# Prologue of a cross-attention and mixture-of-experts kernel: an order of its own for each engine, and fp32 raw scores for the first unit

## The chip, the cores and the metric

The kernel runs on one core of a Trainium2 chip. Its time is the device time of one execution in microseconds (us), the median over several runs. TensorE is the matrix engine (PE in the profile, PEld its weight loads), VectorE is DVE, ScalarE is ACT, GpSimd is POOL, and SyncE (SP) issues most of the DMAs. Rows whose engine ends in q (SPq, ACTq) are instructions that issue DMAs.

## What is computed

The input `x` is 8 x 256 x 512, with `ctx` of the same shape and a mask of 8 x 512. Cut to what matters:

```
y = x + attention(layernorm(x), ctx)   # 16 heads of 16 dims over the 256 channels, 512 positions
    q = Wq @ ln(x) + bq;  k = Wk @ ctx + bk;  v = Wv @ ctx + bv
    dot = q.T @ k / 4;  dot = mask * dot - (1 - mask) * 1e6
    out = (softmax(dot) * mask) @ v
out = y + experts(layernorm(y))        # 8 experts, top 2 by a gate; silu(g) * u, then w2
```

## The kernel before

The attention works on 16 **units** of 128 channels (8 heads of 16 dims), two to a batch. A unit goes through a pipeline: load `x`, normalize, project queries and keys (fp32 matmuls into a PSUM tile, `project`, line 1017), add bias and mask (`projection_out`, line 812, into `qkf`), and split each fp32 value in three bf16 **parts** (GpSimd's `part`, lines 554 to 562). The parts go out to `stack_d` in DRAM (`keep_split`, line 370) and come back **stacked** (`stack`, lines 352 and 355) in `qk`, so that one bf16 matmul over 97 rows gives a raw score in nearly full precision, the mask row among them. `raw_scores` (line 985) fills a tile of two such matmuls, and VectorE takes the maximum of each row (`maximum`, line 731). A unit has 16 such tiles, `m` 0 to 15. TensorE transposes the maxima (line 1072), VectorE splits them in three rows (lines 742 to 748), and SP writes these into `qk` (line 454). Then the real scores follow (`scores`, line 972, 100 rows), ScalarE takes the exponential (line 629), and `product` (line 1001) multiplies by the values (`values`, line 1028). Head by head, unit u+1's maxima are taken while unit u's scores run.

Each engine has its own program, and every one of them is the same loop: `unit(u)` for `u` from `FIRST` = -5 to `LAST` = 18, in which the parts that have no unit yet are left out. In iteration `u`, TensorE runs unit u's scores in eight steps `s`, the raw scores of unit u+1 from `m` = 4 on and of unit u+2 for `m` < 4, values of unit u+1 after step 1, queries of unit u+3 after step 3 and keys of unit u+3 after step 7. Raw scores for `m` = 0 stand in step 6, and `m` = 8 in step 2 of the next iteration; each waits for one half of the unit's stack. PSUM tiles come from a ring of two (`NSLOT`), so that a tile waits until the one two before it is read. The list `TILES` gives their order and the numbers that semaphores count.

Iterations -5 to -1 are the prologue. There GpSimd first fills constant ones (lines 486 and 488), waits for all 13 constant loads, and only then takes its first reciprocal root (lines 534 and 536). VectorE and TensorE wait likewise for all constants. SP writes padding rows of 1.3 MB (lines 468 and 470) between its iterations -3 and -2. The experts come after the attention, and lines above 1110 are theirs.

## Time and profile before

| | us |
|---|---|
| median of 3 runs | 930.77 (930.25 to 931.76) |
| profiled execution | 934.06 |
| its span, first to last instruction | 932.3 |

The attention ends near 620 us and the experts take the rest. In the rows below a timeline line gives the start and the length in us, then engine, line, operation, output<-input, the number of instructions merged, and in brackets how long the engine idled before and what ended that. Busy time is pipelined for TensorE, so the starts of neighbouring matmuls tell more than their lengths.

### The profile page before, as it was taken

Reading aid. Unit: us, or ns where it says so; the run is one execution under the profiler, and the core shown is the slowest. Engines: PE = TensorE matmul, PEld = TensorE weight load, DVE = VectorE, ACT = ScalarE, POOL = GpSimd, SP = SyncE. Lnnn points to the kernel's source line nnn. Section 1 sums busy time; section 2 is a strip of 40 time slices with the busy share of each in tenths; the row PEclk is TensorE's granted clock in tenths of the full one; section 3 lists DMA queues with packets and bytes.
Section 4 is the critical chain, followed back from the end, with each engine's and each line's share of the span. In section 5 each row is a group of like instructions: output and inputs, shape, how many; then the busy total and the mean of one; then the engine's idle time right before and its main releaser. Section 6 shows DMA issues by size and latency. Waiting matters only on the chain. (4 is left out here: it accounts for less than half of the span.)

```text
span 932.3 us, 12897 instructions
## 1 busy us (share of the span) xinstructions
PE 804.5 (86%) x3737; PEld 368.1 (39%) x3738; DVE 543.6 (58%) x1038; ACT 316.7 (34%) x615; POOL 376.7 (40%) x396
## 2 busy tenths in 40 slices
PE   2177999999999999999999888219999999999994
PEld 1022333333333333333333232216666666665662
DVE  2167878887888888887778772232333333323332
ACT  0002565556565555655566567000000000000000
POOL 4634354557556655755575142410122222212122
PEclk9667999999999999999999999559999999999998
DMA  4553386667666765856564423242465455463342
GB/s 122 169 171 94 120 246 185 205 190 231 197 208 208 235 197 172 278 153 188 169 204 148 115 83 104 103 148 47 69 159 131 88 147 116 113 160 68 68 68 34
DMA packets 84287, 137.69 MB, mean 148 GB/s; under 512 B 14600, under 2 KB 40520, under 8 KB 84240
## 3 DMA queue, kind: packets, MB, share of 16 engines
q1 hardware_dynamic: 68512, 107.97, 38.5%
q0 software_dynamic: 7744, 17.86, 10.1%
q10 hardware_dynamic: 7984, 11.28, 4.3%
q8 instruction: 23, 0.38, 0.2%
q14 instruction: 24, 0.20, 0.1%
HBM read 77.34 MB, written 59.36 MB: 147 GB/s over the span
## 5 line engine op out<-in xcount | busy, mean ns | idle before, releaser
L731 DVE TENSOR_REDUCE mx<-tile 128x2 f32<-128x1024 f32 x256 | 308.7, 1216 | 67.4 <-PE tile L985 63.8
L629 ACT ACTIVATE pr<-sc 128x512 f32<-128x512 f32 x512 | 268.9, 601 | 193.3 <-PE sc L972 190.5
L985 PE MATMUL tile<-qk 97*128 97x512 bf16 x512 | 158.1, 392 | 49.3 <-DVE mx L731 23.6
L972 PE MATMUL sc<-qk 100*128 100x512 bf16 x512 | 155.1, 383 | 7.4 <-DMA qk<-mxt 4.8
L1289 POOL DMA_INDIRECT out_dram<-y,ids x36 | 56.1, 1558 | 259.7 <-DVE ids L1210 255.7
L1001 PE MATMUL pvb<-pr,vp 128*32 128x512 f32 x1024 | 138.0, 611 | 0.0
L985 PEld LDWEIGHTS tile<-qk 97*128 97x128 bf16 x512 | 36.4, 98 | 189.2 <-DVE mx L731 84.0
L1269 ACT ACTIVATE sg<-gp 128x352 f32<-128x352 f32 x36 | 16.7, 463 | 266.5 <-PE gp L1310 266.5
L1342 PE MATMUL dp<-wring,at 128*128 (+1 forms) x216 | 98.8, 593 | 1.7 <-DVE at L1220 1.7
L1310 PE MATMUL gp<-wring,xtile 128*128 x288 | 93.5, 468 | 1.1 <-DVE meta L1201 1.1
L554 POOL TENSOR_SCALAR parts<-qkf 128x512 bf16<-128x512 f32 x32 | 48.4, 1511 | 110.8 <-DVE qkf L812 109.9
L1310 PE MATMUL up<-wring,xtile 128*128 x288 | 91.2, 459 | 0.0
L972 PEld LDWEIGHTS sc<-qk 100*128 100x128 bf16 x512 | 49.5, 100 | 91.0 <-ACT pr L629 39.0
L1310 PEld LDWEIGHTS gp<-wring,xtile 128*128 128x128 f32 x288 | 55.6, 193 | 41.9 <-issue 19.3
L1226 DVE TENSOR_SCALAR y<-dp,metay 128x512 f32<-128x512 f32 x36 | 27.0, 751 | 71.4 <-PE dp L1342 71.4
L1310 PEld LDWEIGHTS up<-wring,xtile 128*128 128x128 f32 x288 | 51.9, 190 | 22.8
L1342 PEld LDWEIGHTS dp<-wring,at 128*128 128x128 f32 (+1 forms) x216 | 41.0, 190 | 43.8 <-issue 36.3
L1235 DVE TENSOR_TENSOR ac<-sg,up 128x352 f32<-128x352 f32 x36 | 18.8, 521 | 55.4 <-PE up L1310 29.8
L1017 PE MATMUL tile<-xh,wq_s 128*128 128x512 f32 x64 | 34.3, 662 | 18.8 <-DVE xh L674 17.9
L559 POOL TENSOR_SCALAR parts<-rest 128x512 bf16<-128x512 f32 x32 | 47.7, 1491 | 2.8
L1218 DVE COPY at<-atp 128x256 f32<-128x256 f32 x36 | 15.3, 424 | 55.2 <-PE atp L1332 49.0
L569 POOL TENSOR_TENSOR att<-num,rb 128x512 f32<-128x512 f32 x16 | 20.3, 1268 | 59.7 <-DMA rb<-recip_d 59.7
(118 smaller groups left out, 745.2 us busy)
## 6 DMA issues: line engine op xcount, KB each, us to landing
qk<-stack_d SPq DMA_DIRECT2D x32, 768.0 KB
stack_d<-parts SPq DMA_DIRECT2D x32, 384.0 KB, 2.6
wring<-w_dram SPq DMA_DIRECT2D x32, 352.0 KB, 6.2
xl<-routed_d ACTq DMA_DIRECT2D x38, 257.0 KB, 2.7
stack_d<-parts SPq DMA_DIRECT2D x32, 256.0 KB, 2.9
pv_d<-ov SPq DMA_DIRECT2D x32, 256.0 KB, 4.3
xin<-x_dram SPq DMA_DIRECT2D x16, 256.0 KB, 5.4
cin<-ctxt_dram SPq DMA_DIRECT2D x8, 512.0 KB, 6.4
```

Source lines behind the costliest of these rows:

```text
L554: pool.tensor_scalar(parts[:, side, 0, :], src, 1.0, None, ALU.mult).then_inc(done.sem, 1)
L559: pool.tensor_scalar(parts[:, side, 1, :], rest[:, side, :], 1.0, None, ALU.mult).then_inc(done.sem, 1)
L629: nc.scalar.activation(pr[s % 2][:, j, :], sc[(32 * u + 4 * s + j) % NSC][:, :], ACT.Exp, scale=SCALE).then_inc(exped.sem, 1)
L731: dve.tensor_reduce(mx[:, half(w), 2 * j:2 * j + 2], t[:, :, :], X, ALU.max, negate=True).then_inc(drained.sem, 1)
L972: nc.tensor.matmul(sc[(32 * u + 4 * s + j) % NSC][:, :], ks[half(u)][0:ALL_ROWS, h, c * P:c * P + P], qs[half(u)][0:ALL_ROWS, h, :], start ...
L985: last = nc.tensor.matmul(t[:, i, :], qs[half(w)][0:RAW_ROWS, h, c * P:c * P + P], ks[half(w)][0:RAW_ROWS, h, :], start=True, stop=True)
L1001: last = nc.tensor.matmul(pvb[32 * i:32 * i + 32, :], vp[half(u)][:, c, 4 * g + i, :], pr[s % 2][:, i, :], start=(c == 0), stop=(c == 3))
L1017: last = nc.tensor.matmul(t[:, 0, :], weight[:, c, half(w) * P:half(w) * P + P], source[:, parity(w), c, :], start=(c == 0), stop=(c == 1))
L1226: dve.tensor_scalar(y[:, k, :], dp[:, :], metay[:, k, 0:1], None, ALU.mult).then_inc(y_made, 1)
L1289: pool.indirect_dma_start(out, bass.IndirectOffsetOnAxis(ap=ids[:, k, :], axis=0), y[:, k, :], None, compute_op=ALU.add).then_inc(y_added, 16)
L1310: last = nc.tensor.matmul(dst[:, 0:I], xt[k][:, c, :], wring[:, bass.ds(off + (c * 2 * I + o), I)], start=(c == 0), stop=(c == 3))
L1342: last = nc.tensor.matmul(dp[:, :], at[0:w, c, :], wring[0:w, bass.ds(off + (W1N + c * T), T)], start=(c == 0), stop=(c == len(ICHUNKS) - 1))
```

## The change

The loop from `FIRST` to -1 is replaced, on every engine, by a list written out by hand. The constants that are needed first (`early`) are loaded first, with semaphores of their own, and each engine waits for these alone. Queries and keys of units 0 and 1 are projected one after another. The queries and keys of unit 0 are copied in fp32, a head to each group of 32 partitions, with a mask row below (`heads_in`, into `qf`, which lies in the buffer `pr0`). The raw scores of unit 0 come from these (`first_raw`): 17 rows of fp32 each, two heads to a tile. Meanwhile GpSimd splits the queries of unit 0, and VectorE the keys (`key_parts`), and they are stacked for the real scores as before. The queries and keys of unit 2 are projected inside iteration 0, after steps 0 and 2. The padding rows are written after iteration 1.

```
+        max_ = [(n, ("max", m)) for m in pairs_of(n, s)]
+        ev += max_[:1]
+        if s == 7 and has(n - 2):
+            ev.append((n, "ranks"))
+        ev += max_[1:]
+        ev += [(n, name) for name in fillers(n, s)]
+        if n == 0 and s == 0:
+            ev.append((-1, "q"))
+        if n == 0 and s == 2:
+            ev.append((-1, "k"))
...
+FIRST_TILES = ([(-3, "q"), (-3, "k"), (-2, "q"), (-2, "k")] + [(-2, ("max", m)) for m in range(LEAD)]
+               + [(-1, ("max", m)) for m in range(LEAD, NPAIR)] + [(-1, "maxT"), (-1, ("max", 0)), (-1, ("max", 1)),
+               (-1, "v"), (-1, ("max", 2)), (-1, ("max", 3))])
+TILES = FIRST_TILES + [tile for n in range(LAST + 1) for tile in tile_events(n)]
...
+        qf = pr[0][:, :, :].rearrange("p (g s) t -> p g s t", g=2)
+        mf = ge[:, :, :].rearrange("o a b -> o (a b)")[:, 0:2 * T].rearrange("o (s t) -> o s t", s=2)
...
+        early = ((io[:, :], iotas, io_in),
+                 (wq_s[:, :, :], wq.rearrange("(c p) o -> p c o", p=P), wq_in),
+                 (bqk[:, 0, :], bq, wq_in),
+                 (wk_s[:, :, :], wk.rearrange("(c p) o -> p c o", p=P), wk_in),
+                 (bqk[:, 1, :], bk, wk_in),
+                 (mall[:, :], mask, mask_in))
...
+        def heads_in(eng, heads):
+
+            eng.wait_ge(drained.sem, drained.at(-3, "k"))
+            for h in heads:
+                at = GROUP * (h % 4)
+                eng.dma_start(qf[at:at + D, h // 4, :, :], qkf[h::UH, 0, :, :]).then_inc(qf_in, 16)
...
+                if u == 0:
+                    keep_split(-1, 0)
...
+            load_x(-5)
+            load_x(-4)
+            load_ctx(-3)
+            sp.wait_ge(mask_made, 2)
+            sp.dma_start(mf_d[:, :], mf[:, :, :]).then_inc(mf_kept, 16)
+            load_x(-3)
+            load_x(-2)
+            sp.wait_ge(mf_kept, 16)
+            for g in range(2):
+                sp.dma_start(qf[D::GROUP, g, :, :], mf_d.rearrange("(o s) t -> o s t", o=1).broadcast_to([4, 2, T])
+                             ).then_inc(qf_in, 16)
+            heads_in(sp, range(4))
+            sp.wait_ge(mask_made, 4)
             for side in range(2):
                 sp.dma_start(mrow_d[:, side], mrow[:, side:side + 1, :].broadcast_to([B, 4, T])
                              ).then_inc(mrow_kept, 16)
+            keep_split(-3, 0)
+            keep_split(-2, 1)
             sp.wait_ge(mrow_kept, 32)
-            for i in range(4):
-                sp.dma_start(routed_d[E * CAP + i * P:E * CAP + (i + 1) * P, :], pad[:, :]
-                             ).then_inc(padded, 16)
-            sp.dma_start(out[TOKENS:TOKENS + P, :], pad[:, 0:T]).then_inc(padded, 16)
-            for u in range(-2, LAST + 1):
+            sp.wait_ge(ones_made, 1)
+            sp.wait_ge(split_kept[0].sem, split_kept[0].at(-3, "k"))
+            sp.wait_ge(split_kept[1].sem, split_kept[1].at(-2, "k"))
+            stack(0, 0)
+            stack(0, 1)
+            keep_split(-2, 0)
+            load_ctx(-1)
+            load_x(-1)
+            keep_split(-1, 1)
+            sp.wait_ge(ones_made, 3)
+            sp.wait_ge(split_kept[0].sem, split_kept[0].at(-2, "k"))
+            sp.wait_ge(split_kept[1].sem, split_kept[1].at(-1, "k"))
+            for g in range(2):
+                sp.wait_ge(stacked[g].sem, stacked[g].at(g - 2, "g"))
+                stack(1, g)
+            keep_maxima(-1)
+            for u in range(LAST + 1):
                 unit(u)
+                if u == 1:
+                    sp.wait_ge(const_made, MADE)
+                    pads()
 
...
+            ones_of(0)
+            pool.wait_ge(io_in, 16)
+            batch_rstd(-5)
+            batch_rstd(-4)
+            pool.wait_ge(normed.sem, normed.at(-4, "n"))
+            ones_of(1)
+            part(-3, 0)
+            batch_rstd(-3)
+            batch_rstd(-2)
+            part(-2, 0)
+            part(-1, 1)
+            values_out(-1)
+            batch_rstd(-1)
+            part(-1, 0)
+            for u in range(LAST + 1):
...
+            for dst, src, loaded in early:
+                act.dma_start(dst, src).then_inc(loaded, 16)
             for dst, src in const:
                 act.dma_start(dst, src).then_inc(const_loaded, 16)
+            heads_in(act, range(4, 8))
...
-                dve.tensor_reduce(mx[:, half(w), 2 * j:2 * j + 2], t[:, :, :], X, ALU.max, negate=True
+                cols = mx[:, half(w), 2 * j:2 * j + 2]
+                if w == 0:
+                    at = 4 * (4 * (j // 8) + 2 - 2 * (j % 2)) + j % 8 // 2
+                    cols = mx[:, 0, at:at + 5:4]
+                dve.tensor_reduce(cols, t[:, :, :], X, ALU.max, negate=True
                                   ).then_inc(drained.sem, 1)
...
+                if u == 0:
+                    projection_out(-1, 0)
...
+                if u == 0:
+                    projection_out(-1, 1)
...
+            def key_parts(u):
+
+                w = u + 2
+                src = qkf[:, half(w), 1, :]
+                dve.wait_ge(drained.sem, drained.at(u - 1, "k"))
+                dve.tensor_reduce(parts[:, 1, 0, :], src.rearrange("p (t o) -> p t o", o=1), X, ALU.max
+                                  ).then_inc(split[1].sem, 1)
+                dve.wait_ge(split[1].sem, split[1].at(u, 0))
+                dve.tensor_tensor(rest[:, 1, :], src, parts[:, 1, 0, :], ALU.subtract).then_inc(split[1].sem, 1)
+                dve.wait_ge(split[1].sem, split[1].at(u, 1))
+                dve.tensor_reduce(parts[:, 1, 1, :], rest[:, 1, :].rearrange("p (t o) -> p t o", o=1), X, ALU.max
+                                  ).then_inc(split[1].sem, 1)
+                dve.wait_ge(split[1].sem, split[1].at(u, 2))
+                dve.tensor_tensor(parts[:, 1, 2, :], rest[:, 1, :], parts[:, 1, 1, :], ALU.subtract
+                                  ).then_inc(split[1].sem, 1)
+
...
-            dve.wait_ge(const_loaded, CONST)
+            for u in (-5, -4):
+                batch_stats(u, 0)
+                batch_stats(u, 1)
+            normalize(-5)
+            normalize(-4)
+            dve.wait_ge(io_in, 16)
             dve.tensor_copy(first[:, :], io[0:1, 16:24]).then_inc(const_made, 1)
             dve.tensor_scalar(pad[:, T + 1:T + 2], io[:, 0:1], float(TOKENS), None, ALU.add
                               ).then_inc(const_made, 1)
+            dve.wait_ge(mask_in, 16)
+            dve.tensor_copy(mf[:, 0, :], mall[0:1, :]).then_inc(mask_made, 1)
+            dve.tensor_scalar(mf[:, 1, :], mall[0:1, :], 1.0, NEG / SCALE, ALU.subtract, ALU.mult
+                              ).then_inc(mask_made, 1)
+            dve.wait_ge(wq_in, 32)
+            projection_out(-3, 0)
+            dve.wait_ge(wk_in, 32)
+            projection_out(-3, 1)
+            dve.tensor_copy(mrow[:, 0, :], mall[:, :]).then_inc(mask_made, 1)
+            dve.tensor_scalar(mrow[:, 1, :], mall[:, :], 1.0, NEG / SCALE, ALU.subtract, ALU.mult
+                              ).then_inc(mask_made, 1)
+            key_parts(-2)
+            projection_out(-2, 0)
+            projection_out(-2, 1)
+            for j in range(LEAD):
+                maximum(-2, j)
+            for u in (-3, -2):
+                batch_stats(u, 0)
+                batch_stats(u, 1)
+            dve.wait_ge(const_loaded, CONST)
             dve.tensor_copy(upper[:, :], utf[:, :]).then_inc(const_made, 1)
-            dve.tensor_copy(mrow[:, 0, :], mall[:, :]).then_inc(const_made, 1)
-            dve.tensor_scalar(mrow[:, 1, :], mall[:, :], 1.0, NEG / SCALE, ALU.subtract, ALU.mult
-                              ).then_inc(const_made, 1)
             dve.wait_ge(const_made, MADE)
-            for u in range(FIRST + 1, LAST + 1):
+            for j in range(LEAD, 8):
+                maximum(-1, j)
+            normalize(-3)
+            normalize(-2)
+            for j in range(8, NPAIR):
+                maximum(-1, j)
+            split_maxima(-1)
+            maximum(-1, 0)
+            maximum(-1, 1)
+            values_out(-1)
+            maximum(-1, 2)
+            maximum(-1, 3)
+            batch_stats(-1, 0)
+            batch_stats(-1, 1)
+            normalize(-1)
+            for u in range(LAST + 1):
...
+                if u == 0 and c == 0 and j == 0:
+                    pe.wait_ge(stacked[g].sem, stacked[g].at(g - 2, "g"))
...
+            def first_raw(u, m):
+
+                t = slot(u, ("max", m))
+                g, c, j = m // 8, m % 8 // 2, 2 - 2 * (m % 2)
+                for i in range(2):
+                    at = GROUP * (j + i)
+                    both = qf[at:at + D + 1, g, :, :]
+                    last = nc.tensor.matmul(t[:, i, :], both[:, 0, c * P:c * P + P], both[:, 1, :],
+                                            start=True, stop=True)
                 last.then_inc(ready.sem, 1)
...
+                    if u == 0 and s == 0:
+                        project(-1, 0)
+                    if u == 0 and s == 2:
+                        project(-1, 1)
...
+            pe.wait_ge(wq_in, 32)
+            project(-3, 0)
+            pe.wait_ge(wk_in, 32)
+            project(-3, 1)
+            project(-2, 0)
+            project(-2, 1)
+            pe.wait_ge(qf_in, 10 * 16)
+            for m in range(LEAD):
+                first_raw(-2, m)
+            for m in range(LEAD, NPAIR):
+                first_raw(-1, m)
+            pe.wait_ge(const_loaded, CONST)
+            pe.wait_ge(const_made, MADE)
+            pe.wait_ge(ones_made, 4)
+            transpose_maxima(-1)
+            raw_scores(-1, 0)
+            raw_scores(-1, 1)
+            values(-1)
+            raw_scores(-1, 2)
+            raw_scores(-1, 3)
+            for u in range(LAST + 1):
                 unit(u)
```

Left out of the diff: the semaphores, the counting class that takes a list, `keep_maxima` (the former end of SP's `unit`, as a function) and the names passed on.

On TensorE, from the start to the first score (`sc`) of unit 0; `tile` is the PSUM ring, `qk` the stacked parts. Before:

```order
L1017 MATMUL tile<-xh,wq_s 128x512 x2
L1017 MATMUL tile<-cin,wk_s 128x512 x2
L1017 MATMUL tile<-xh,wq_s 128x512 x2
L985 MATMUL tile<-qk 128x512 x8
L1017 MATMUL tile<-cin,wk_s 128x512 x2
L985 MATMUL tile<-qk 128x512 x8
L1028 MATMUL tile<-wv_s,cin 128x128 x8
L985 MATMUL tile<-qk 128x512 x8
L1017 MATMUL tile<-xh,wq_s 128x512 x2
L985 MATMUL tile<-qk 128x512 x12
L1072 MATMUL tile<-idf,mx 32x128
```

After; `pr` holds the fp32 heads:

```order
L1164 MATMUL tile<-cin,wk_s 128x512 x2
L1164 MATMUL tile<-xh,wq_s 128x512 x2
L1164 MATMUL tile<-cin,wk_s 128x512 x2
L1132 MATMUL tile<-pr 128x512 x32
L1219 MATMUL tile<-idf,mx 32x128
L1121 MATMUL tile<-qk 128x512 x4
L1175 MATMUL tile<-wv_s,cin 128x128 x8
L1121 MATMUL tile<-qk 128x512 x4
L1108 MATMUL sc<-qk 128x512 x2
```

The 32 matmuls of unit 0's raw scores no longer read `qk`, the second pair of projections moved ahead of them, and unit 2's query projection is gone from this stretch.

On SP, the last DMAs ahead of iteration 0 (down to `qk<-mxt`, the rows of maxima) and the first of it. Before:

```order
L352 DMA qk<-stack_d 96x2x2048
L355 DMA qk<-mrow_d 1x2x2048
L370 DMA stack_d<-parts 128x3x512
L370 DMA stack_d<-parts 128x2x512
L370 DMA stack_d<-parts 128x512
L454 DMA qk<-mxt 1x32x128 x3
L352 DMA qk<-stack_d 96x2x2048
L355 DMA qk<-mrow_d 1x2x2048
L344 DMA xin<-x_dram 128x512
```

After:

```order
L376 DMA qk<-stack_d 96x2x2048
L379 DMA qk<-mrow_d 1x2x2048
L376 DMA qk<-stack_d 96x2x2048
L379 DMA qk<-mrow_d 1x2x2048
L448 DMA qk<-mxt 1x32x128 x3
L368 DMA xin<-x_dram 128x512
L394 DMA stack_d<-parts 128x3x512
L394 DMA stack_d<-parts 128x2x512
L394 DMA stack_d<-parts 128x512
L394 DMA stack_d<-parts 128x3x512
L394 DMA stack_d<-parts 128x2x512
L394 DMA stack_d<-parts 128x512
```

Both halves of unit 1's stack now stand ahead of the maxima, and the query parts of unit 2 are stored in iteration 0, just ahead of its key parts.

## Rows read from the trace of the kernel before

**Rows 1.** busy time by window; columns: stretch, length, busy us of each engine, clock, DMA.

```profile
90.00:100.00 10.00, 10.00 (x64) 4.36 (x63) 7.82 (x8) 6.23 (x13) 3.65 (x3) 1.00 0.25 82
```

**Rows 2.** waits, first 90 us; engine and line, releaser: us in total, times, longest.

```profile
ACT L629 <- PE sc L972: 86.6, 1, 86.6
```

**Rows 3.** timeline, first 25 us: start, us, engine, line, out<-in, count, idle before.

```profile
0.73 3.51 POOL L486 MEMSET qk<- 32x4096 bf16 x1 [0.29 <-POOLq L1400]
...
3.65 0.69 DVE L659 BATCH_NORM_STATS2 ln<-xin 128x6 f32<-128x512 f32 x1 [3.65 <-DMA xin<-x_dram]
...
12.15 0.23 POOL L534 TENSOR_SCALAR ln<-ln 128x1 f32<-128x1 f32 x1 [3.17 <-issue]
...
13.08 0.55 DVE L674 TENSOR_SCALAR xh<-xin,ln 128x512 f32<-128x512 f32 x1 [8.52 <-POOL ln L536]
...
17.88 3.75 PE L1017 MATMUL tile<-xh,wq_s 128*128 128x512 f32 x4 [17.88 <-DVE xh L674]
...
24.34 0.75 DVE L812 SCALAR_TENSOR_TENSOR qkf<-tile,bqk,mb 128x512 f32<-128x512 f32 x1 [1.47 <-PE tile L1017]
```

**Rows 4.** timeline, 33 to 68 us, SP's queue and TensorE: pads, stacks.

```profile
33.27 1.83 SPq L468 DMA_DIRECT2D routed_d<-pad  x4
...
42.47 0.33 SPq L352 DMA_DIRECT2D qk<-stack_d  x1
...
48.34 1.89 PE L985 MATMUL tile<-qk 97*128 97x512 bf16 x4 [22.32 <-DMA qk<-mrow_d]
...
63.27 1.57 SPq L370 DMA_DIRECT2D stack_d<-parts  x3
...
67.03 0.33 SPq L352 DMA_DIRECT2D qk<-stack_d  x1
```

**Rows 5.** timeline, unit 0 and the start of unit 1: S, parts, m0, U1.

```profile
86.06 1.06 PE L972 MATMUL sc<-qk 100*128 100x512 bf16 x2
...
87.15 1.49 POOL L554 TENSOR_SCALAR parts<-qkf 128x512 bf16<-128x512 f32 x1 [8.67 <-DVE qkf L812]
...
92.77 1.58 SPq L370 DMA_DIRECT2D stack_d<-parts  x3
...
97.07 0.60 PE L972 MATMUL sc<-qk 100*128 100x512 bf16 x2
...
107.72 0.59 PE L985 MATMUL tile<-qk 97*128 97x512 bf16 x2
...
116.16 0.60 PE L972 MATMUL sc<-qk 100*128 100x512 bf16 x2 [0.27 <-DMA qk<-mxt]
```

**Rows 6.** transfers, first 90 us: issuing queue, count, KB, us to landing.

```profile
qk<-mxt SPq DMA_DIRECT2D x3, 8.0 KB, 1.9
```

**Rows 7.** timeline, VectorE and GpSimd side by side at 42 us.

```profile
42.37 0.94 DVE L674 TENSOR_SCALAR xh<-xin,ln 128x512 f32<-128x512 f32 x1 [0.36 <-POOL ln L536]
42.42 1.51 POOL L554 TENSOR_SCALAR parts<-qkf 128x512 bf16<-128x512 f32 x1
```

**Rows 8.** timeline: values, maxima transposed and issued, value product, one projection.

```profile
61.26 3.53 PE L1028 MATMUL tile<-wv_s,cin 128*128 128x128 f32 x16 [0.52 <-DVE mx L731]
...
79.10 0.37 PE L1072 MATMUL tile<-idf,mx 128*32 128x128 f32 x1 [0.31 <-DVE mx L731]
...
81.17 1.85 SPq L454 DMA_DIRECT2D qk<-mxt  x3
...
91.01 1.07 PE L1001 MATMUL pvb<-pr,vp 128*32 128x512 f32 x8
...
99.90 1.88 PE L1017 MATMUL tile<-xh,wq_s 128*128 128x512 f32 x4
```

**Rows 9.** groups by line, first 90 us: VectorE's reduction, count, busy, mean ns.

```profile
L731 DVE TENSOR_REDUCE mx<-tile 128x2 f32<-128x1024 f32 x22 | 25.8, 1217 | 7.6 <-PE tile L985 7.4
```

**Rows 10.** timeline, units 1 and 2: second stack issued, its first use.

```profile
143.91 0.58 SPq L352 DMA_DIRECT2D qk<-stack_d  x1
...
153.07 0.60 PE L985 MATMUL tile<-qk 97*128 97x512 bf16 x2
```

91 lines of the change are left out of this document (41 added, 50 removed).

## The prediction

> **What bounds the kernel now.** I read the busy time by window first, then the waits of the first 90 us, then the timeline of that stretch. Once the units run, TensorE is busy for 10.00 of 10 us at the full clock [rows 1], and the change leaves units 2 to 15 and the expert part as they are. So the only question is how much earlier the steady units begin. The waits show an empty start: ScalarE waits 86.6 us for the first score [rows 2], and ahead of that stand two long pauses of TensorE, 17.88 us until the normalized tokens [rows 3] and 22.32 us until the stacked parts [rows 4]. I count in three marks: S, the first score matmul of unit 0 (86.06), m0, the first raw-score matmul of unit 2 inside unit 0 (107.72), and U1, the first score of unit 1 (116.16) [rows 5]. The gain is what U1 moves.
>
> **Start, per engine.** Before, the first use of the reciprocal root on GpSimd waits for all thirteen constants and both halves of memsets, until 12.15 [rows 3], and TensorE starts at 17.88. After, one memset pair stands ahead (0.73 + 3.51, and 0.5 for the second: 4.8), x is in at 3.65, and only `io` is needed. What the 3.17 us of "issue" ahead of 12.15 are made of (a wait for constants, or GpSimd's own preparation) the row does not tell; the bounds are 4.9 and 8.1. I take 5.6, nearer the lower, because the wait for thirteen transfers of constants lay in that same stretch. Two reciprocal roots at 13.08 - 12.15 = 0.93 and 0.55 for the second normalization bring TensorE to **8.1** (10.6 at the bound). The weights must have landed too: cost between 0 and 4, taken as 0, for they are now second and fourth in their queue.
>
> **Projections to fp32 heads.** VectorE reads the keys 6.5 us after TensorE starts (24.34 against 17.88 [rows 3]), and the queries about 2.7 earlier: keys are out at 8.1 + 6.5 + 0.75 = 15.3. Then eight small transfers, four on each of SP's and ScalarE's queues, at 0.46 us of issue (four in 1.83 [rows 4]): 17.1. Landing of such a transfer is not in the trace; it lies between 1.9 us (8 KB of maxima [rows 6]) and 5.9 (a stack [rows 4]); I take 2.8, nearer the small one: **19.9**. VectorE meanwhile writes the mask rows (0.8), the four key-part steps (no row; about the 0.75 of the projection's eviction each, so 3.0) and the eviction of unit 1's queries (0.75): 19.9 as well. Neither hides the other's slip.
>
> Those key-part steps run beside GpSimd's query parts (from 12.8 to 18.5), and the trace shows that such neighbours slow each other: a normalization of VectorE took 0.94 beside a part step of GpSimd that began 0.05 later [rows 7], where it took 0.55 alone [rows 3]. By that row two of the four steps lose up to 0.4 each, which the 0.75 apiece covers; if instead each of two steps waits for a whole step of GpSimd, 1.2 to 1.5, the fp32 tiles start 2.6 later. That is rival (b) below. The Trainium skill (SBUF — State Buffer, SBUF: two separate sides) states the second: a VectorE instruction with two SBUF inputs and a GpSimd instruction that reads SBUF exclude each other for the whole instruction. By that rule the time is 918.2.
>
> **Sixteen raw tiles in fp32.** Each tile is two heads of 512 columns, two passes each. One fp32 pass takes 0.43 us at full clock (four in 1.88 [rows 8]) and twice that at half (four in 3.75 [rows 3]). One after another they would be 1.72 per tile, or 3.44 at half. Heads in different groups of partitions may run together. The trace has no row groups, only column groups: eight passes of the value product in 1.07 where 3.44 would be serial [rows 8], 3.2 times faster. By that row a pair takes 0.9 and VectorE's reduction, 1.2 [rows 9], is last. TensorE has worked from 8.1 to about 18, so it is at the full clock. Bounds 1.2 and 3.44 per tile; I take 1.2. (Serial passes at full clock, 1.72, would end the reductions at 48.6 and move S by 1.5.) First tile read at 21.8; four reductions to 26.6; two statistics (0.69 [rows 3] and 0.2 each) to 28.4; twelve more reductions (14.4), a cast and two normalizations (1.3) to **44.1**.
>
> **What is late next: unit 1's stack.** GpSimd's key and query parts for unit 1 stand behind the reciprocal roots of units 2 and 3, and those wait for statistics that VectorE takes only after four reductions (28.4). So: 29.3; query parts 5.7, key parts 5.7 (one set, start to SP's issue, is 92.77 - 87.15 = 5.6 [rows 5]): 40.7. SP stores them and then issues the load 3.8 us later (67.03 - 63.27 [rows 4]), plus 0.7 because context, mask and x are ahead in the queue: 45.2. From load issue to TensorE is 48.34 - 42.47 = 5.9 [rows 4]: **51.1**. TensorE has idled from 44, so I price the rest at half clock: raw pairs and values as before (four bf16 passes in 1.89 [rows 4], values 3.53 [rows 8], reductions between them): 7.6; at full clock 5.9. **S = 58** (57 to 58.7). The maxima of unit 0 are hidden: 44.1 + 2.1 (81.17 - 79.10 [rows 8]) = 46.2, SP free at 47.2, issue 1.85, landed by 54 even behind both stacks. The 1.3 MB of pads, which SP issued from 33.27 [rows 4], are no longer in the way.
>
> **Inside unit 0: part of it is given back.** Unit 2's query and key projections, once in the prologue, now stand in unit 0 after steps 0 and 2, where TensorE has no free time: 2 x 1.88. VectorE also takes its statistics and waits for GpSimd's root before it reads on: 1.5. So TensorE reaches m0 at S + 21.7 + 5.3 = 85.0. But m0 needs unit 2's stack. The key projection ends step 2: S + 11.0 (97.07 - 86.06 [rows 5]) + 1.9 + 1.5 = 72.4, evicted at 75.2; parts 5.7: 80.9; store and load 3.8: 84.7; landing 5.9: **90.6**. TensorE stands 5.6 us, with the scores of unit 0 queued behind the raw matmul, so ScalarE stands too. From m0 to U1 8.4 [rows 5]: 99.0. After such a pause matmuls run at half clock for a while (0 to 2.5 us, taken as 1): U1 = 100.0, against 116.16: 16.2 gained.
>
> **Pads in unit 1.** Five DMAs (2.4 us of SP's time) and 1.3 MB now stand ahead of unit 3's second stack. Before, its issue at 143.91 is needed at 153.07 [rows 10]: 9.2 us for a 5.9 us load, 3.3 spare. Issue 2.4 later and queued behind 1.3 MB: 0 to 3, taken as 1. All else in the steady units costs nothing by count: the same instructions in the same order.
>
> **Sum**: 16.2 - 1 = 15.2. The profiled run took 934.06 us around a span of 932.3; the median of the runs is 930.77. I take the difference off the median: 915.6; a profiled run would show about 919.
>
> **Rivals.**
> (a) The start is held: weights or GpSimd's first root arrive as late as their bounds. Everything shifts by 2.5 to 4: **919**. For: the transfers of the first 10 us crowd each other. Against: the needed ones now lead.
> (b) The key-part steps on VectorE are shut out while GpSimd's steps run: 2.6 later, **918**. For: 0.94 in place of 0.55. Against: that row lost 0.4, not a whole step.
> (c) Row groups run one after another and at half clock in the first four tiles, on which the statistics, GpSimd and the stack of unit 1 hang: 4 x 3.44 + 1.2 instead of 6.7, about 8 later: **924**. For: such fp32 matmuls are new here. Against: TensorE comes to them from 10 us of work.
> (d) The stall at m0 is absent, because parts, store and load overlap better than added: 5.6 + 1 back: **909**. Against: each link is a wait on the last.
> (e) Slower: all sixteen tiles serial at half clock, 55.0 us. The last reduction is at 76.1, S at 83.5, and with 42 to U1 it is 125.5, 9.3 late, plus 1 of pads: **941**. It decides from 2.8 us per tile on. Against: so busy a TensorE was at full clock in the steady windows.
> (f) The change does not do what it says: the raw matmuls still wait as long as the stacks do, no time moves, **930 to 931**. The order of instructions speaks against it: no wait for a stack stands ahead of the fp32 tiles.
>
> **How the numbers follow.** Forecast 0.56 (its own range 911 to 920), (a) 0.10, (b) 0.10, (c) 0.07, (d) 0.11, (e) 0.04, (f) 0.02. The predicted time is the forecast's. The range 907 to 923 leaves out (c), (e) and (f), 0.13. Faster by over 0.2% (1.9 us, about what a measurement can tell from no change) 0.94, within it 0.02, slower 0.04.
>
> **What would show it.** First projection near 8; fp32 raw tiles from 20, one reduction after another at 1.2; last reduction near 44; TensorE idle to 51 on the load of `qk`; S near 58; a wait of 4 to 7 us before a raw matmul in unit 0; U1 near 100; units from 2 on as long as before. It would be wrong if the tiles take over 1.5 us each, if unit 0 shows no such wait, or if the later units change.

## The result and the profile after

The changed kernel takes 926.0 us (median of 12 runs, 923.2 to 928.9), the kernel before on the same chip 930.8: a ratio of 0.9946, 95% interval 0.9930 to 0.9962. It is 5 us faster. I had predicted 915.6, with a range from 907 to 923. The profiled run of the changed kernel took 925.97 us, with a span of 924.2. (In "The change", the list of TensorE's new order lacks its first line, unit 0's query projection, `tile<-xh,wq_s`, which starts at 7.78.)

The timeline of the new start, a selection of lines from several engines; columns as in [rows 3].

```profile
15.83 1.55 POOL L619 TENSOR_SCALAR parts<-rest 128x512 bf16<-128x512 f32 x1
16.65 0.69 DVE L1020 TENSOR_TENSOR rest<-qkf,parts 128x512 f32<-128x512 f32 x1
17.46 1.16 POOL L622 TENSOR_TENSOR parts<-rest,parts 128x512 bf16<-128x512 f32 x1
18.10 1.07 DVE L1025 TENSOR_TENSOR parts<-rest,parts 128x512 bf16<-128x512 f32 x1
20.89 1.14 PE L1132 MATMUL tile<-pr 17*128 17x512 f32 x8 [3.89 <-DMA pr<-qkf]
23.34 3.21 PE L1132 MATMUL tile<-pr 17*128 17x512 f32 x8 [1.32 <-DVE mx L812]
25.47 2.36 DVE L812 TENSOR_REDUCE mx<-tile 128x2 f32<-128x1024 f32 x2 [1.05 <-PE tile L1132]
27.74 0.68 DVE L736 BATCH_NORM_STATS2 ln<-xin 128x6 f32<-128x512 f32 x1
28.73 0.23 POOL L594 TENSOR_SCALAR ln<-ln 128x1 f32<-128x1 f32 x1 [10.11 <-DVE ln L739]
30.54 1.52 POOL L614 TENSOR_SCALAR parts<-qkf 128x512 bf16<-128x512 f32 x1
30.87 3.21 PE L1132 MATMUL tile<-pr 17*128 17x512 f32 x8 [0.92 <-DVE mx L812]
45.62 0.33 SPq L376 DMA_DIRECT2D qk<-stack_d  x1
51.39 1.89 PE L1121 MATMUL tile<-qk 97*128 97x512 bf16 x4 [1.14 <-DMA qk<-mrow_d]
59.13 0.93 PE L1108 MATMUL sc<-qk 100*128 100x512 bf16 x2
```

Up to here the time is almost as forecast. The fp32 tiles start at 20.89 (19.9 predicted), unit 1's stack is read at 51.39 (51.1), and the first score S stands at 59.13 (58), where [rows 5] has 86.06. The gain of 27 us at S is real. Most of it is lost again behind S. The second part of the timeline is unit 0:

```profile
64.31 3.78 PE L1164 MATMUL tile<-xh,wq_s 128*128 128x512 f32 x4 [1.69 <-DVE mx L812]
...
76.40 1.88 PE L1164 MATMUL tile<-cin,wk_s 128*128 128x512 f32 x4
...
89.01 0.33 SPq L376 DMA_DIRECT2D qk<-stack_d  x1
...
94.88 1.04 PE L1121 MATMUL tile<-qk 97*128 97x512 bf16 x2 [5.94 <-DMA qk<-mrow_d]
...
96.38 1.08 ACT L703 ACTIVATE pr<-sc 128x512 f32<-128x512 f32 x2 [6.54 <-PE sc L1108]
```

TensorE waits 5.94 us for unit 2's stack, with the scores of unit 0 queued behind it, and ScalarE 6.54. The busy time by window shows the clock that TensorE was granted (the columns are those of [rows 1]; the clock is the last but two, 1.00 is 2.4 GHz and 0.50 is 1.2 GHz):

```profile
12.00:22.00 10.00, 6.11 (x20) 2.22 (x18) 7.38 (x10) 0.00 (x0) 5.55 (x4) 1.00 0.81 191
22.00:59.00 37.00, 30.00 (x85) 11.53 (x82) 26.91 (x31) 0.00 (x0) 12.90 (x13) 0.50 0.63 187
64.30:68.10 3.80, 3.79 (x5) 1.47 (x6) 1.09 (x1) 0.00 (x0) 0.00 (x0) 0.50 0.00 0
...
94.00:101.00 7.00, 5.86 (x18) 1.30 (x19) 2.58 (x3) 1.80 (x4) 0.00 (x0) 0.52 0.33 117
```

TensorE stands at 2.4 GHz up to the first two fp32 tiles and at 1.2 GHz for the other fourteen, again for unit 2's query projection, and again after the wait in unit 0. Ahead of the fall at 22 it had waited 3.89 us for the fp32 heads and then worked for 1.14.

What a unit costs can be read off the starts of its exponentials on ScalarE (one number from each trace, in us; unit 1's exponentials start 0.4 after U1). There is a second profile of either kernel. The last two columns are the length of unit 2, and what units 3 to 12 take above 31.83 each, the length of an undisturbed one:

| kernel | unit 0 | unit 1 | length of unit 2 | excess of units 3 to 12 | first expert product |
|---|---|---|---|---|---|
| before | 88.08 | 116.59 | 31.82 | 2.3 | 626.4 |
| before, second profile | 86.30 | 114.92 | 31.82 | 4.0 | 624.1 |
| changed | 61.15 | 105.48 | 33.42 | 5.6 | 618.1 |
| changed, second profile | 62.14 | 103.49 | 33.96 | 5.5 | 617.7 |

So 25.5 us are gained at unit 0, 11.3 are left at unit 1, 9.5 behind unit 2 and 7.3 at the experts, whose part is as long as before (305.9 and 306.4 before, 306.1 and 306.7 after). The medians differ by 5 and not by 7: the profiled runs of the kernel before (934.06 and 932.25) lie above its medians (930.8 to 932.7) or at their upper end. These pieces therefore rest on two traces of each kernel, and differences of under 2 us between them can be those of single runs.

### The profile page after: what moved, and what is told of

The parts are those of the page before. It is cut to its first block and busy times, and to the rows that moved or that the text cites. A ratio compares the mean times of both kernels' runs of the same rounds, so it can differ in the third digit from the quotient of the medians.

```text
span 924.2 us, 12981 instructions
## 1 busy us (share of the span) xinstructions
PE 815.2 (88%) x3769; PEld 372.9 (40%) x3770; DVE 551.8 (60%) x1044; ACT 317.0 (34%) x615; POOL 371.3 (40%) x392
## 5 line engine op out<-in xcount | busy, mean ns | idle before, releaser
L1121 PE MATMUL tile<-qk 97*128 97x512 bf16 x480 | 147.3, 390 | 27.2 <-DVE mx L812 16.1
L1121 PEld LDWEIGHTS tile<-qk 97*128 97x128 bf16 x480 | 34.1, 98 | 158.4 <-DVE mx L812 74.5
L1481 PEld LDWEIGHTS gp<-wring,xtile 128*128 128x128 f32 x288 | 55.7, 194 | 41.8 <-issue 19.3
L1164 PE MATMUL tile<-xh,wq_s 128*128 128x512 f32 x64 | 35.0, 674 | 10.2 <-DMA bqk<-bq_dram 7.8
```

The lines of the kernel that those rows point to most:

```text
L1121: last = nc.tensor.matmul(t[:, i, :], qs[half(w)][0:RAW_ROWS, h, c * P:c * P + P], ks[half(w)][0:RAW_ROWS, h, :], start=True, stop=True)
L1164: last = nc.tensor.matmul(t[:, 0, :], weight[:, c, half(w) * P:half(w) * P + P], source[:, parity(w), c, :], start=(c == 0), stop=(c == 1))
L1481: last = nc.tensor.matmul(dst[:, 0:I], xt[k][:, c, :], wring[:, bass.ds(off + (c * 2 * I + o), I)], start=(c == 0), stop=(c == 3))
```

## The experiments

The ratios are to the kernel before on the same chip, with 95% intervals. Kernels that ran together form a group. In the first group the changed kernel, run again, has a median of 927.9 and a ratio of 0.9957 (0.9935 to 0.9980), and the kernel before 932.7.

### The changed kernel again

> The changed kernel once more, unedited. In its first trace unit 0's exponentials start 26.9 us earlier than before and unit 1's 11.1 us, but the first expert product only 8.3 us: units 2, 5, 7 and 8 are 1.6, 2.3, 0.7 and 1.8 us longer than the kernel before has them, and the kernel before has one such unit (3, 2.0 us). In units 5 and 8 the next unit's first score waits for the landing of the rows of maxima. Theory (chance): these late landings fall on other units each time, so units 5 and 8 are back at 31.85 us here, one to three other units are long, and unit 2 alone keeps 33.4 us (the pads). Rival (caused by the change): units 2, 5, 7 and 8 are long again by the same 1.6, 2.3, 0.7 and 1.8 us. Time by both: 0.993 to 0.996 of the kernel before.

Units 5 and 8 are long in both traces, so chance is refuted for them. Unit 5 takes 33.60 us (34.31 the first time), unit 8 33.67 (33.64), unit 7 32.37 (32.51). The transfers tell why for units 5 and 8. The timeline around the start of unit 6 and, for comparison, of unit 5 in the first trace:

```profile
228.23 1.83 SPq L448 DMA_DIRECT2D qk<-mxt  x3
231.56 0.60 PE L1108 MATMUL sc<-qk 100*128 100x512 bf16 x2
260.56 1.85 SPq L448 DMA_DIRECT2D qk<-mxt  x3
265.87 0.61 PE L1108 MATMUL sc<-qk 100*128 100x512 bf16 x2 [1.81 <-DMA qk<-mxt]
```

Three small transfers carry the rows of maxima. Normally the first score follows their issue by 3.33 us, here by 5.31. The packets by queue (count, MB, share of 16 engines) from 2.3 us after the issue, first for unit 5, in the 0.5 us from 230.5:

```profile
q1 hardware_dynamic: 48, 0.01, 8.4%
```

then for unit 6, in the 0.4 us from 262.9:

```profile
q8 instruction: 1, 0.02, 22.9%
q1 hardware_dynamic: 45, 0.01, 9.9%
```

Here 3 of the 48 packets are missing, a sixteenth, which is one DMA engine's part, and there is one packet of instructions, of 16 KB. It starts at 263.17 and takes 1.47 us; the three missing packets follow it at 264.62 to 264.68, and the score 1.2 us later. The page of the changed kernel has 23 such packets:

```profile
q8 instruction: 23, 0.38, 0.2%
```

Between two of them lie 257 records of TensorE on average, and a steady unit has 347. This points to TensorE's own code, loaded 16 KB at a time by the engines that carry the data. If so, its place in a unit follows from the number of TensorE instructions ahead, about the same in every run of a kernel and another in a kernel whose TensorE code is longer or shorter. The experiments that move the code, below, bear that out.

Unit 7 in the first trace and unit 3 in the second are long for another reason. The timeline of the first trace, in unit 7 and, for comparison, in unit 10:

```profile
324.63 1.26 POOL L637 TENSOR_TENSOR x<-att,xr 128x512 f32<-128x512 f32 x1
325.14 0.77 DVE L860 TENSOR_TENSOR selb<-sel 128x8 bf16<-128x8 f32 x1
...
423.20 0.15 DVE L860 TENSOR_TENSOR selb<-sel 128x8 bf16<-128x8 f32 x1
```

A tiny step of VectorE, which adds two pieces of `sel` in SBUF, ends 0.02 us after GpSimd's step that was running when it began. In the sixteen traces this step took over 0.3 us 23 times, and each time it ended 0.02 to 0.03 us after a GpSimd TENSOR_TENSOR. It stands just ahead of the steps that split the next unit's maxima, and of the seven steady units that have it and no late rows of maxima, six are longer by the same time within 0.2 us (unit 7 here by 0.68). GpSimd comes late there since it waits for a DMA, `rb<-recip_d`; why that lands late no run here tells.

### Raw scores from the stack

```diff
-            pe.wait_ge(qf_in, 10 * 16)
             for m in range(LEAD):
-                first_raw(-2, m)
+                raw_scores(-2, m)
             for m in range(LEAD, NPAIR):
-                first_raw(-1, m)
+                raw_scores(-1, m)
```

Not shown here: the ten loads of heads and mask rows and the store of the mask row go too.

> The changed kernel without its fp32 raw scores: unit 0's 16 tiles of raw scores are computed from the stack, in bf16 with 97 rows, in the new prologue, and the loads of heads and mask row into the fp32 operand are gone. Nothing else of the prologue changes. Theory (the fp32 operands bring next to nothing): the stack of unit 0 has landed at 29 us, or some 3 us earlier without the ten loads ahead of it on SP; from there 16 maxima of 1.18 us on DVE (18.9), statistics and normalisation between them (3.9) and no wait for TensorE at full clock end at 49 to 52 us, against 49.6 with fp32 tiles at 1.7 us each. Since the stack of unit 1 lands at 51.4 us either way, unit 0's first score stays within 1 us of 58.7, and the time within 1.5 us of the changed kernel. Rival (they are what the change is worth, as my prediction had it): tiles that start 8 us later end 5 to 8 us later, the first score comes at 63 to 66 us, and the kernel is 4 to 7 us slower than the changed one.

933.1 us, ratio 1.000 (0.998 to 1.002): all of the change's gain is gone. The rival was right on the time (5.2 us above the changed kernel), but not on the way there: the first score comes at 68.3, later than the 63 to 66 that it gave. The timeline:

```profile
31.55 1.89 PE L1110 MATMUL tile<-qk 97*128 97x512 bf16 x4 [14.35 <-DMA qk<-mrow_d]
38.24 0.23 POOL L587 TENSOR_SCALAR ln<-ln 128x1 f32<-128x1 f32 x1 [19.31 <-DVE ln L731]
40.05 1.52 POOL L607 TENSOR_SCALAR parts<-qkf 128x512 bf16<-128x512 f32 x1
```

The tiles start 10.7 us later, yet the sixteen maxima end only 5.7 later (55.3, 49.6), since VectorE then runs without waits. Unit 0 starts 8 to 9 us later (70.1): GpSimd waits 19.3 us for statistics that stand behind the first four maxima, and unit 1's parts stand behind GpSimd's roots.

### The order on GpSimd, with and without fp32

```diff
             part(-3, 0)
+            part(-2, 0)
+            part(-1, 1)
             batch_rstd(-3)
             batch_rstd(-2)
-            part(-2, 0)
-            part(-1, 1)
```

> The changed kernel with the inverse roots of units 2 and 3 behind the parts of unit 1 on POOL, instead of ahead of them. In the changed kernel POOL waits 10 us for their statistics, which DVE takes only after the first four maxima, so the parts of unit 1 start at 30.5 us. Theory (the first four maxima matter through POOL's order): the parts run from 20 to 31, the stack of unit 1 is usable at about 40 and not 51.4, but TensorE then comes from the maxima's transposition at 49.9, so the first score of unit 0 gains 1.0 to 1.5 us, and the time 1 to 1.5 us. Rival (POOL beside DVE's reductions slows both): the fp32 tiles or the parts get longer and the gain is nothing or negative.

926.8 us, 0.9926 (0.9900 to 0.9952), against 0.9946 and 0.9957 of the changed kernel: no difference that these intervals tell. The parts of unit 1 end at 34.6 instead of 41.8, and unit 0 starts at 61.3: the sixteen maxima end at 51.2 and hold TensorE now. Unit 1 starts at 106.5, 2.0 later than the mean of the changed kernel's two traces, with the clock at half for longer (window as above):

```profile
90.00:104.00 14.00, 9.49 (x30) 1.93 (x31) 4.63 (x7) 3.26 (x6) 1.62 (x2) 0.51 0.40 128
```

After the wait for unit 2's stack it stays at half for 13.7 us here, for 6.8 in the changed kernel.

The same with the tiles from the stack, both edits together:

> The kernel without the fp32 raw scores (tiles from the stack) with the same new order on POOL. Without the new order it starts unit 0 some 8 to 9 us after the changed kernel: its four first maxima start at 32.6 instead of 22.1, and through the statistics the parts of unit 1 start at 40.1 instead of 30.5. Theory (half of what the fp32 tiles are worth is the POOL order): with the order cured the first score is bound by the 16 maxima alone, which end at 55.3 against 49.6, so unit 0 starts 4 to 5 us after the changed kernel's, at 65.5 to 66.5 us, and the time is 1.5 to 4 us above the changed kernel's. Rival (the chain of maxima alone is worth it all): unit 0 starts at 68 or later, and the time stays 5 us above.

927.5 us, 0.9949 (0.9922 to 0.9976). The tiles from the stack are read at 31.25, and unit 0 starts at 63.86, 2.2 us after the mean of the changed kernel's two traces and not 8.4. Unit 1 starts at 106.51, the same as with fp32 and this order. So the fp32 operands are worth 5.2 us (927.9 against 933.1) in the changed order of GpSimd, and 0.7 by the medians, less than the intervals can tell, once two small instructions there stand two places later. That unit 1 starts at the same time in the two traces is luck, however: TensorE's wait for unit 2's stack ends 2.0 us later with the tiles from the stack (96.27 against 94.26), and the clock then stands at half for 3.4 us and not for 13.7. With the same clock some 2 us could be left of the operands' worth.

### The pads

```diff
             stack(0, 1)
+            sp.wait_ge(const_made, MADE)
+            pads()
             keep_split(-2, 0)
...
-                if u == 1:
-                    sp.wait_ge(const_made, MADE)
-                    pads()
```

> The changed kernel with its five stores of pads issued in the prologue, where SP waits from 27.1 to 36.1 us for the query parts, and not ahead of unit 3's stack inside unit 1. Theory (the pads delay the stack): unit 2 takes 31.85 us instead of 33.42, and the time is 1.6 us below the changed kernel's; unit 0 starts where it did. Rival (the pads lie in SP's slack, and unit 2 was long by chance): unit 2 is unchanged in kind, and the time is within 0.5 us of the changed kernel's.

925.1 us, 0.9916 (0.9888 to 0.9945), 2.8 below the changed kernel of the same group. Unit 2 takes 31.83 us and unit 0 starts where it did (62.48), so the theory holds, with 1.6 to 2.1 us for unit 2. The rest of the 2.8 fits unit 5, which takes 31.86 in this trace: its code transfer starts 2.93 us after the issue of the maxima rows, 0.3 later than in the two traces of the changed kernel, and misses them.

### Both projections of unit 2 in one step

```diff
-            ev.append((-1, "q"))
-        if n == 0 and s == 2:
-            ev.append((-1, "k"))
+            ev += [(-1, "q"), (-1, "k")]
...
                     if u == 0 and s == 0:
                         project(-1, 0)
-                    if u == 0 and s == 2:
                         project(-1, 1)
```

> The changed kernel with unit 2's k projection right behind its q projection in the first score step of unit 0, instead of two steps later; DVE takes both out one after the other. Theory (the key parts set the stall): the key parts start when the query parts end (74.5 us) and not at 79.2, so the stack of unit 2 lands 4.7 us earlier, TensorE's wait for it in unit 0 shrinks from 5.9 to about 1 to 2 us, and unit 1 starts 3.5 to 4.5 us earlier: 921.5 to 923 us where the changed kernel has 926. Rival (the projections at half clock set it): a second projection of 3.8 us in the same step delays the scores around it, and of the gain 2 us or less is left.

919.7 us, 0.9852 (0.9825 to 0.9878): 8.2 us below the changed kernel, about twice what the theory gave. The timeline and one window:

```profile
83.54 0.33 SPq L374 DMA_DIRECT2D qk<-stack_d  x1
...
89.48 0.60 PE L1118 MATMUL tile<-qk 97*128 97x512 bf16 x2 [0.60 <-DMA qk<-mrow_d]
```

```profile
84.00:98.00 14.00, 12.63 (x67) 3.79 (x67) 11.01 (x14) 8.17 (x17) 5.22 (x4) 1.00 0.47 138
```

The stack is loaded 5.5 us earlier, TensorE waits 0.6 us, and the clock stays at full, where it had fallen for 7 us before. Unit 1 starts at 97.94, 6.5 us before the mean of the changed kernel, where the waits are 5.1 us shorter. The wait thus cost its own length and 1 to 2 us more, and the matmuls at half clock behind it account for that. (VectorE takes the two projections out one behind the other as well.) The profiled run is the slowest of its six, at 922.65: its experts start only 3.6 us before those of the changed kernel, since units 13 and 14 take 2.6 longer together. So unit 1 shows 6.5 of the 8.2 us, and the trace does not show where the rest comes from.

### TensorE's code moved

Tiny matmuls ahead of the first raw scores, while TensorE waits, are there only to move its code: 12 of them are 48 instructions, 5 are 20.

```diff
+            for _ in range(12):
+                nc.tensor.matmul(pvb[0:32, 0:32], wq_s[:, 0, 0:32], wq_s[:, 0, 0:32], start=True, stop=True)
             pe.wait_ge(qf_in, 10 * 16)
```

> The changed kernel with twelve tiny fp32 matmuls (32 x 32, into the product's bank before its first use) while TensorE waits for the heads: 48 more TensorE instructions ahead of the loop, nothing else. In both traces of the changed kernel a code transfer of 16 KB on queue q8, one for every 256 or so TensorE records, starts 2.6 us after the issue of the rows of maxima for units 6 and 9 and lasts 1.3 to 1.5 us, and the first score of these units comes 1.8 to 2.0 us later than in the others; in the kernel before the same shows once, for unit 4. Theory (the code of TensorE is loaded by the same DMA engines, and its place in the unit is set by the number of instructions ahead): with 48 instructions more no such transfer falls beside the maxima rows of units 3 to 12, units 5 and 8 take 31.9 us instead of 34.0 and 33.7, and the time is about 3.5 us below the changed kernel's. Rival (late landings have another cause that happens to coincide): units 5 and 8 stay long, the time stays.

928.6 us, 0.9947 (0.9926 to 0.9967): no gain. Units 5 and 8 take 31.98 and 31.92 us, as the theory had it, but unit 10 takes 33.62 and unit 13 31.64 (31.85 and 29.6 to 29.8 in the changed kernel). The timeline at the starts of units 6 and 11:

```profile
264.68 1.84 SPq L448 DMA_DIRECT2D qk<-mxt  x3
268.00 0.60 PE L1108 MATMUL sc<-qk 100*128 100x512 bf16 x2
...
423.97 1.83 SPq L448 DMA_DIRECT2D qk<-mxt  x3
429.07 0.60 PE L1108 MATMUL sc<-qk 100*128 100x512 bf16 x2 [1.60 <-DMA qk<-mxt]
```

A code transfer starts 2.62 us after the second issue; at the first one it starts 1.5 us ahead of the issue. The cause is shown, my bounds of the hits were too narrow. Unit 1 also started 4.3 us late (108.8): the clock fell for 10.2 us after the wait in unit 0.

The same with `range(5)`:

> As the kernel with twelve matmuls, but with five, 20 more TensorE instructions. A unit in the steady part has 347 records, and a code transfer comes every 256. By that count the transfer that stands 16 records behind the first score of unit 3 moves to 4 records ahead of it, and the one at 1 record ahead of unit 6's to 21, at the edge. Theory: unit 2 gets long by another 1.3 to 2 us (it has 33.4 to 34.0 with the pads), unit 8 is back at 31.9, unit 5 either way; the time is 1 to 3 us below the changed kernel's or the same. Rival (coincidence): units 5 and 8 stay long and unit 2 as it was.

925.1 us, 0.9919 (0.9889 to 0.9950). Unit 2 takes 36.44 us, more than the 1.3 to 2 on top that I expected: its code transfer, 2.31 us after the issue, makes the score 1.0 late, TensorE waits 1.85 for the stack behind the pads, and the clock stands at half for 3.4 us from 144.0. Unit 5, the one at the edge, takes 33.00; unit 8 is at 31.94.

```profile
165.95 1.83 SPq L448 DMA_DIRECT2D qk<-mxt  x3
170.30 0.60 PE L1108 MATMUL sc<-qk 100*128 100x512 bf16 x2 [0.85 <-DMA qk<-mxt]
```

Which units are hit came out as predicted. The time is lower than the changed kernel's (0.9957 and 0.9946), but the intervals overlap, so they do not tell it from no change, which I had also allowed.

In the kernel before, six such matmuls:

```diff
+            pe.wait_ge(const_loaded, CONST)
+            for _ in range(6):
+                nc.tensor.matmul(pvb[0:32, 0:32], wq_s[:, 0, 0:32], wq_s[:, 0, 0:32], start=True, stop=True)
             pe.wait_ge(const_made, MADE)
```

> The kernel before with six tiny fp32 matmuls, 24 more TensorE instructions, ahead of everything else on TensorE, while it waits for the constants. Its unit 3 is long (33.84 us) since a code transfer falls on the rows of maxima for unit 4, 4 records ahead of its first score by the count. Theory: with 24 more it stands 28 ahead, no other falls there, unit 3 takes 31.9 us, and the time is 2 us below the kernel before (0.998). So part of what the change lost in its steady units is the place of its code, which an edit that does nothing gives and takes. Rival: unit 3 stays long.

930.9 us, 0.9992 (0.9973 to 1.0011). Unit 3 takes 32.20 us instead of 33.84, but unit 11 is hit instead (33.38). The mechanism is right. The interval does not tell the forecast 0.998 from no change, and with one hit moved and not removed there was nothing to gain.

The kernel before, unedited:

> The kernel before once more, unedited, for a second profile. Its first profiled run took 934.06 us where the medians of its runs are 930.8 to 932.7. Theory (the start of unit 1 and the place of the code hits are fixed, single waits vary): unit 1 starts within 1 us of 116.6, unit 3 is long again by 1.3 to 2.0 us, and the run takes 930 to 933. Rival (where transfers land varies from run to run): another unit is long, or none.

932.25 us in one run. Unit 1 starts at 114.9, 1.7 earlier than in the first trace and not within the 1 us that I gave. Unit 3 is long again (33.77), and unit 6 as well (33.49), where the first trace has 31.84: there its code transfer started 2.91 us after the issue, here 2.53.

```profile
301.91 1.83 SPq L454 DMA_DIRECT2D qk<-mxt  x3
306.89 0.61 PE L972 MATMUL sc<-qk 100*128 100x512 bf16 x2 [1.48 <-DMA qk<-mxt]
```

So both theory and rival hold a part: the place is fixed, and at the edge a few tenths of a microsecond decide.

### Combined

`best` has both projections in one step, the pads in the prologue, the new order on GpSimd, and

```diff
+            nc.scalar.activation(ex[:, :], idf[:, 0:1], ACT.Exp)
...
                     projection_out(-1, 0)
+                    projection_out(-1, 1)
+                    key_parts(0)
```

GpSimd leaves out unit 2's key parts in return.

> The changed kernel with the two projections of unit 2 together in unit 0's first step (alone that gave 0.985 of the kernel before), and four things more: unit 2's key parts on DVE and not POOL, the pads in the prologue, the roots behind unit 1's parts on POOL, and one exponential of a constant ahead of unit 0, which loads ACT's table while it waits. Theory (the wait for unit 2's stack in unit 0 is the largest piece, and half clock comes behind it): the 1.7 us of that wait left go, as the key parts no longer follow the query parts; pads 1.6, order on POOL 0 to 1, table 1.2. Unit 1's exponentials start at 94 to 96 us (97.9 with the projections alone, 103.5 to 105.5 in the changed kernel), unit 2 takes 31.85, and the time is 914 to 917, 0.980 of the kernel before. Rival (key parts on DVE hold back its maxima and so the scores): unit 1 starts at 98 or later, and only pads and table are gained, 0.983.

919.8 us, 0.9874 (0.9850 to 0.9898). The rival is right, and the time is even above its 0.983: unit 1 starts at 100.2, 2.2 us later than with the projections alone, although unit 0 starts 2.4 earlier. VectorE's four instructions hold its maxima, TensorE waits for it, and the projection of the values behind it runs at half clock (1.95 us at full):

```profile
74.85 3.56 PE L1175 MATMUL tile<-wv_s,cin 128*128 128x128 f32 x16 [2.29 <-DVE mx L810]
```

`best_values` adds one move on TensorE, with its counterparts on VectorE and in the list of tiles:

```diff
+            pe.wait_ge(const_loaded, CONST)
+            values(-1)
             pe.wait_ge(qf_in, 10 * 16)
...
             raw_scores(-1, 1)
-            values(-1)
```

> As the last, and unit 0's values are projected before the first raw scores, while TensorE waits for the heads, and no longer at half clock (3.8 us, 53.7 to 57.5) between the raw scores of unit 1. Theory (that projection sets the first score): the first score comes 3 to 3.5 us earlier, where the landing of the maxima rows takes over (issue at 51.5 plus 3.3), and the time is 2.5 to 3.5 us lower. Rival (a piece of unit 0 that does not move, the stack of unit 2, takes it back): unit 1 starts where it did, the time stays. That the constants land too late for it (values need them all) would show as a later first fp32 tile.

916.7 us, 0.9849 (0.9822 to 0.9876): 3 us below by the medians of five runs each, with intervals that overlap. Unit 0 starts only 1.6 earlier (57.85), since the maxima end 1 us later, and unit 1 2.1 earlier.

The same with eleven of the tiny matmuls behind `values(-1)`:

> As the last with eleven tiny fp32 matmuls, 44 more TensorE instructions, ahead of the first raw scores. Without them the code transfers for units 6 and 9 fall on the rows of maxima, as in the changed kernel. By the hits seen so far (a transfer that stands 8 behind to 21 ahead of the first score, counted in TensorE records of units of 347) none of units 3 to 12 is hit with 44 more, the nearest being at 28 ahead and 12 behind. Theory: units 5 and 8 take 31.9 us, none takes over 32.5, and the time is 2.5 to 3.5 us below the kernel without them. Rival: another unit is hit (the edges are not known that well), and the gain is 0 to 2 us.

917.0 us, 0.9830 (0.9799 to 0.9860), the same as without. Unit 8 is down from 33.27 to 32.14, units 2 and 13 are hit instead (33.67 and 31.24, for 31.82 and 29.56).

The last edit takes the key parts off VectorE again:

```diff
                     projection_out(-1, 1)
-                    key_parts(0)
```

> The kernel best_values with the key parts of unit 2 on POOL again. Theory (four more instructions on DVE in unit 0 cost more than the earlier stack saves: TensorE waits 2.3 to 2.9 us for DVE there, the granted clock falls once more, and the values of unit 1 take 3.6 us at half clock instead of 1.9): unit 0 goes from 40.2 back to 36 to 37 us, unit 1's exponentials start at 93.5 to 95 and not at 98.0, and the time is 3 to 4 us below best_values, 912.5 to 914. Rival (unit 0 is bound by something the two share): unit 1 starts at 97 or later, the time stays at 916 to 917.

914.0 us, 0.9807 (0.9777 to 0.9836): 17 us below the kernel before and, by the ratios, 13 to 14 below the changed one. Unit 0 takes 38.4 us, more than the 36 to 37 expected, but unit 1 starts at 95.4, so the theory holds against its rival. The clock stands at half from 21 to 66 here, into unit 0, and at full through the steady units. ScalarE's first exponential follows the first score at once, without the 1.28 us of table load that the changed kernel has there:

```profile
56.34 1.02 PE L1105 MATMUL sc<-qk 100*128 100x512 bf16 x2
56.98 1.09 ACT L700 ACTIVATE pr<-sc 128x512 f32<-128x512 f32 x2 [24.89 <-PE sc L1105]
```

## Why the prediction was wrong

**Start, heads.** Right. TensorE starts at 7.8 (8.1), the fp32 tiles at 20.9 (19.9). Rival (a) did not come. Rival (b), VectorE held by GpSimd for two whole steps, did not come either, but what it describes is real. The row of VectorE at 16.65 above has two inputs in SBUF, starts in the middle of GpSimd's TENSOR_SCALAR of 15.83, and takes 0.69 us. By the Trainium skill (SBUF — State Buffer, SBUF: two separate sides) it would have waited until 17.4. This row does not agree, nor do the same rows of six other traces. Beside a TENSOR_TENSOR of GpSimd the traces do agree: the last key-part step, at 18.10, takes 1.07 and ends 0.55 after GpSimd's step of 17.46 (0.55 in the second trace too, where it takes 0.81), and there are the 23 long steps of 0.16 us under "The changed kernel again". The lengths of GpSimd's steps are rough in a profile.

**Sixteen tiles at 1.2 us.** Wrong: 1.7 each. The row groups do run together: eight passes, two tiles, in 3.21 at half clock, where [rows 8] and [rows 3] have 0.43 per pass at full and 0.94 at half, so 7.5 one after another; the first eight, at full clock, take 1.14. But I had the clock at full because TensorE came from ten us of work. It had stopped at 17.0 and waited 3.89 us for the heads, and the clock was at half from 22 to 59. At half clock a tile is 2.1 us from its first matmul to its reduction (23.34 to 25.47), the reduction takes 1.2, and only then is its place in the ring of two free for the next but one: 3.4 us for two tiles. The kernel with tiles from the stack is at half in that stretch too, so half clock there does not need the 17 rows or the fp32. The last reduction came at 49.6, not 44.1, and this cost little: the stack of unit 1 was read at 51.39.

**Unit 1's stack, S.** Right, 51.4 and 59.1 (51.1 and 58 predicted), and I had named what sets them: GpSimd's roots behind the first four maxima. I did not draw the consequence, that the fp32 tiles then pay for most of what they bring through this order alone.

**Unit 0.** The mechanism was right, the sizes were not, and this is the largest miss. The wait has 5.94 us against 5.6 predicted, since both of its ends came some 4 us late. U1 came at 105.1 and not at 100.0: 1.1 of S; 2.8 for unit 2's query projection at half clock (3.78, I took 1.88) and waits around it; 0.4 in SP's issue; and 0.8 for half clock behind the wait, which I had priced at 1 and measured at 1.8. In the second trace the same projection ran at full clock,

```profile
65.63 1.98 PE L1164 MATMUL tile<-xh,wq_s 128*128 128x512 f32 x4 [2.01 <-DVE mx L812]
```

and unit 1 started 2 us earlier. So the mean of two traces is 11.3 gained, 4.9 us less than the 16.2 that I had.

**Pads.** The place was right, the size 1.6 to 2.1 instead of 1.

**Steady units.** This step failed outright. "All else in the steady units costs nothing by count" is true of instructions and wrong of time: on average units 3 to 12 take 2.4 us more than before. Late rows of maxima beside a code transfer, which hit units 5 and 8 here and unit 3, once also unit 6, before, are 1.4 of it (3.7 against 2.3, by the time from the issue of the rows to the score). The other 1.0 lies mostly in unit 7; VectorE's step held by GpSimd is about half of it, and the rest is open.

**The sum.** These are 4.9, 0.9 and 2.4 of the 10.4 us. The last 2 are most likely the base: my estimate was compared with the rows of one run of the kernel before that took 934.06, above its median, and the difference taken off the median. Between the profiled runs the gain is 7.1 us on average, between the medians 4.8. No run separates this from the spread of single runs.

**The rivals.** None described what came. (c) was nearest, at 924, with tiles at half clock, but its price came from passes one after another in the first four tiles, which did not happen, and not from unit 0 or the steady units. My range lacked the sum of several small terms in one direction.

Open is what sets how long the clock stays at half: after the wait in unit 0 it was 6.8 us in five traces, and 3.4, 10.2 and 13.7 in one each, with nearly the same instructions around it. Why unit 1 starts up to 5 us apart (103.5 to 108.8) among kernels with fp32 tiles and that wait is told by it in part only.

## What to carry to other kernels

An early start moves work from an empty prologue into a full loop; price what is moved at half clock as well as at full, and look first for what in the loop waits on it, since a wait there costs its length and the slow matmuls behind it. Before a new kind of operand is built to get one operation earlier, see whether a cheap instruction between that operation and the critical chain can stand elsewhere: moving two roots on GpSimd brought the kernel with tiles from the stack from 933.1 to 927.5, where ten transfers and an fp32 path brought it to 927.9. Where units that should be alike differ by 1 to 2 us, the same ones in each run, compare the start of the code transfers with the last small transfer that each unit waits for, look then for small steps of VectorE that end with a step of GpSimd, and count no edit's gain that is smaller than one such hit from a single trace.

## What the runs showed of the hardware

TensorE's code comes in packets of 16 KB, one per 257 of its records on average, on one of the data's DMA engines for 0.9 to 1.9 us. A small transfer on which a score waits came 1 to 2 us late wherever such a packet started 2.2 to 2.7 us after its issue (26 cases in sixteen traces, no exception), and on time where it started at 2.88 or later (5 cases). Ahead of the last unit, where it started at 1.25 to 1.88, the score was 0.8 to 1.3 us late (8 cases). Edits that only lengthen the code moved this from units 5 and 8 to 10 and 13, or to 2 and 5, and in the kernel before from 3 to 11.

TensorE was granted half clock for 37 us during tiles on which it was busy for 30 of 37 us [the window 22 to 59 above], fed by VectorE, where [rows 1] with 10.00 of 10 is at full.

A VectorE step of 0.16 us with two inputs in SBUF that began inside a TENSOR_TENSOR of GpSimd ended 0.02 to 0.03 us after it, up to 1.04 us late (23 cases over 0.3 us in sixteen traces). A step of 0.69 us with two inputs in SBUF that began inside a TENSOR_SCALAR of GpSimd took no longer (7 traces).
